# Totals in two rounded passes, maxima spread ahead of them, and table work one place forward, in the batch loop of a Perceiver layer

## The reference, cut to what matters

```
kvx = einsum('bsi,oi->bso', cond, w_kv_x)            # cond: 512 rows a batch
kx, vx = split(kvx, 2, axis=-1)
kx = _ln(kx.reshape(b, sc, g, d), kxln_w, kxln_b)    # 8 heads of 128
xout = softmax(q k^T * scale) v                      # 16 query heads
```

```
w = lut[idx]                                         # gate, up and down
```

## Time and profile before

| | us |
|---|---|
| median of 3 runs (427.23 to 427.74) | 427.55 |
| the profiled execution's own time | 427.4 |
| its span, first to last instruction | 425.6 |
| TensorE busy in the span | 414.7 |
| VectorE busy | 347.2 |
| ScalarE busy | 248.8 |

### The profile page before, as it was taken

The page is one execution under the profiler, slowest core; times in us unless marked ns, Lnnn a source line. Parts: engine busy times, 40 slices in busy tenths (PEclk is TensorE's granted clock), DMA queues, the critical chain, the costliest instruction groups (busy, mean ns, idle before and its releaser), DMA issues.

```text
span 425.6 us, 6868 instructions
## 1 busy us (share of the span) xinstructions
PE 414.7 (97%) x2427; PEld 292.2 (69%) x2433; DVE 347.2 (82%) x699; ACT 248.8 (58%) x780; POOL 35.8 (8%) x58
## 2 busy tenths in 40 slices
PE   8999999999999999999999999999999999999897
PEld 3453455788885767778676686785486799837596
DVE  5889999987999899689899998978887787746831
ACT  2478898688547777748986677664505263220220
POOL 0010000040000001100001000010010004101000
PEclk9999999999999999999999999999999999999999
DMA  7599120500002015993554835688337979730000
GB/s 240 226 191 415 39 85 2 199 2 26 27 2 99 1 51 123 201 306 78 132 124 92 198 70 108 155 187 359 74 78 246 390 267 241 151 125 2 2 2 25
DMA packets 14591, 56.80 MB, mean 133 GB/s; under 512 B 1824, under 2 KB 2912, under 8 KB 13280
## 3 DMA queue, kind: packets, MB, share of 16 engines
q1 hardware_dynamic: 11104, 39.31, 25.3%
q0 software_dynamic: 3456, 17.11, 21.4%
HBM read 41.40 MB, written 0.26 MB: 98 GB/s over the span
## 4 chain that ended last, share of the span: by engine, by line
PE 74%; DVE 12%; issue 6%; DMA 4%; ACT 3%; POOL 1%; SPq 0%; DVEq 0%; ACTq 0%; POOLq 0%
PE PS L482 11%; PE PS L1817 10%; PE PS L453 8%; PE PS L454 8%; PE PS L455 8%; PE PS L1846 3%; PE PS L535 3%; PE PS L1287 3%; DMA lutw_dt.float<-luttmp_dt.float 2%; PE PS L1832 2%; DMA raw_dt.float<-in_wk_nat 1%; PE PS L492 1%; PE PS L1153 1%; PE PS L1135 1%; PE PS L1295 1%
## 5 line engine op out<-in xcount | busy, mean ns | idle before, releaser
L605 ACT ACTIVATE sq_dt.float<-PS 128x128 bf16<-128x128 f32 x256 | 67.0, 279 | 27.0 <-PE PS L455 20.5
L482 PE MATMUL PS<-s_dt.float,ctx_ring_dt.float 128*128 128x512 f32 x128 | 57.8, 593 | 0.0
L605 ACT ACTIVATION_READ_ACCUMULATOR sq_dt.float<-PS 128x1 f32 x256 | 53.6, 210 | 0.0
L453 PE MATMUL PS<-wkc_dt.float32r,ctx_hi_dt.float32r 128*128 128x512 f32 x128 | 51.5, 402 | 0.1
L454 PE MATMUL PS<-wkT_dt.float32r,ctx_hi_dt.float32r 128*128 128x512 f32 x128 | 50.0, 390 | 0.0
L455 PE MATMUL PS<-wkc_dt.float32r,ctxT_ring_dt.float32r 128*128 128x512 f32 x128 | 49.9, 390 | 0.0
L687 ACT ACTIVATE luttmp_dt.float<-low_bit_dt.float,vec_dt.float,small_dt.float 128x1536 f32<-128x1536 uint8 x24 | 38.5, 1654 | 8.5 <-DMA lutw_dt.float<-luttmp_dt.float 8.5
L1817 PE MATMUL PS<-wch_dt.float,xs_dt.float 128*128 128x512 f32 x96 | 42.0, 592 | 0.0
L482 PEld LDWEIGHTS PS<-s_dt.float,ctx_ring_dt.float 128*128 128x128 f32 x128 | 23.6, 190 | 23.6 <-issue 23.0
L700 POOL DMA_DIRECT2D lutw_dt.float<-luttmp_dt.float x21 | 18.2, 869 | 234.7 <-DVE luttmp_dt.float L694 234.7
L694 DVE SCALAR_TENSOR_TENSOR luttmp_dt.float<-idx_dt.float,luttmp_dt.float 128x1536 f32<-128x1536 uint8 x21 | 36.6, 1753 | 0.0
(11 more groups left out here) (304 smaller groups left out, 851.3 us busy)
## 6 DMA issues: line engine op xcount, KB each, us to landing
lutw_dt.float<-luttmp_dt.float POOLq DMA_DIRECT2D x21, 768.0 KB, 6.1
wch_dt.float<-in_chunks SPq DMA_DIRECT2D x5, 1024.0 KB, 7.9
ctxT_ring_dt.float<-in_ctxT SPq DMA_DIRECT2D x8, 512.0 KB, 3.4
ctx_ring_dt.float<-in_ctx SPq DMA_DIRECT2D x8, 512.0 KB, 3.9
keysT_dt.float<-in_ctxT SPq DMA_DIRECT2D x8, 512.0 KB, 7.0
keys_dt.float<-in_ctx SPq DMA_DIRECT2D x8, 512.0 KB, 8.0
zu_dt.float<-in_wproj SPq DMA_DIRECT2D x1, 2048.0 KB, 7.2
A_first_dt.float<-in_wproj SPq DMA_DIRECT2D x1, 2048.0 KB, 10.2
```

Source lines behind the costliest of these rows:

```text
L453: nc.tensor.matmul(o, x_hi, hi[:, c, :], start=c == 0, stop=False)
L482: last = nc.tensor.matmul(mix_bank(b, c), keysr[k][:, t, c * 128:c * 128 + 128], sS[k][:, t, :], start=t == 0, stop=t == KT - 1)
L605: last = nc.scalar.activation(sq[:, (4 * hf + g) * D:(4 * hf + g + 1) * D], key_bank(b, 2 * t + hf)[:, g * D:(g + 1) * D], ACT.Square, acc ...
```

## The change

Totals: for batches 1 to 5 the fp32 product with ones becomes two `fp32r` products, of a rounded part `ps_hi` that ScalarE makes and of the rest `ps_lo` that VectorE makes. On TensorE the maxima of steps 2 to 6 are spread before the totals; in step 1 the order stays. On VectorE the sums go ahead of the split of the queries, the subtraction for `ps_lo` takes the place of the first table term, and that term goes behind the shift. GpSimd makes a rounded copy of the ones. Table work: step 1 takes four leaves and terms, steps 2 and 3 three each, step 4 two, and steps 5 to 7 as before.

```diff
-                    total(b - 1)
-                    spread(b)
+                    if isinstance(b, int) and b == 1:
+                        total(0)
+                        spread(1)
+                    else:
+                        spread(b)
+                        total(b - 1)
...
             def total(b):
-                pe.wait_ge(psum_ready, b + 1)
+                split = not (isinstance(b, int) and b in (0, 6, 7))
+                if split:
+                    pe.wait_ge(ps_split, b)
+                else:
+                    pe.wait_ge(psum_ready, b + 1)
...
+                if split:
+                    nc.tensor.matmul(bank(2), ones_r, ps_hi, start=True, stop=False)
+                    nc.tensor.matmul(bank(2), ones_r, ps_lo, start=False, stop=True).then_inc(sum_full, 1)
+                    return
                 nc.tensor.matmul(bank(2), ones, ps2[:, 0, :], start=True, stop=True).then_inc(sum_full, 1)
...
@@ ScalarE, step
-                    for m in range(3):
-                        leaf(act, b - 1, m)
+                    leaf(act, *LUT_TERMS[b][0])
+                    leaf(act, *LUT_TERMS[b][1])
+                if 1 < b < 7:
+                    hi_of_sum(b - 1)
+                for place in LUT_TERMS[b][2:3]:
+                    leaf(act, *place)
                 if prev and more:
                     inverse(b - 1)
+                for place in LUT_TERMS[b][3:]:
+                    leaf(act, *place)
                 if next_context:
                     split_context(b + 2, k)
...
+            def hi_of_sum(b):
+                act.wait_ge(psum_ready, b + 1)
+                nc.scalar.activation(ps_hi, ps2[:, 0, :], ACT.Copy).then_inc(ps_hi_ready, 1)
...
+        LUT_TERMS = {b: [(b - 1, m) for m in range(3)] for b in range(5, 8)}
+        LUT_TERMS[0] = []
+        LUT_TERMS[1] = [(0, 0), (0, 1), (0, 2), (1, 0)]
+        LUT_TERMS[2] = [(1, 1), (1, 2), (2, 0)]
+        LUT_TERMS[3] = [(2, 1), (2, 2), (3, 0)]
+        LUT_TERMS[4] = [(3, 1), (3, 2)]
...
+            pool.wait_ge(ld_const, 16)
+            nc.gpsimd.tensor_copy(ones_r, ones).then_inc(ones_ready, 1)
...
@@ VectorE, step
+                sums(b - 1, 1 - k)
                 if b > 1:
                     lo_of_A(dve, b + 1)
-                sums(b - 1, 1 - k)
                 maxima(b)
                 if b == 1:
                     lo_of_A(dve, 2)
-                term(dve, b - 1, 0)
+                else:
+                    lo_of_sum(b - 1)
                 shift(b, k)
+                term(dve, *LUT_TERMS[b][0])
                 normalise(b - 1, 1 - k)
...
-                term(dve, b - 1, 1)
+                term(dve, *LUT_TERMS[b][1])
...
-                term(dve, b - 1, 2)
+                for place in LUT_TERMS[b][2:]:
+                    term(dve, *place)
...
+            def lo_of_sum(b):
+                dve.wait_ge(ps_hi_ready, b)
+                nc.vector.tensor_tensor(ps_lo, ps2[:, 0, :], ps_hi, ALU.subtract).then_inc(ps_split, 1)
```

More of the change, by code:

```diff
@@ L70 @@
     ("vecs", 5 * NK, LOOP, LAST, "raw"), ("ctx_hi1", CT * NK, LOOP, LAST, "raw"),
+    ("ps_lo", NK, LOOP, LAST, "catc"), ("ps_hi", NK, LOOP, LAST, "raw"),
     ("keys", B * KT * C, TAIL, LATE, "catc"),
@@ L80 @@
     ("rotact", 4 * 1024, LATE, LATE), ("probs", 2 * TT * NK, LATE, LATE),
+    ("ones_r", 128, FRONT, LAST),
 ]
@@ L137, in build @@
         for name in ("zu", "catc", "lutw", "wkc", "wkT", "ctx_hi0", "ctx_hi1", "ctxT_ring", "A_hi", "A", "catx", "A_first", "beta", "gu_a", "gu_b", "gu_hi", "hT_hi",
-                     "hT_lo"):
+                     "hT_lo", "ps_hi", "ps_lo", "ones_r"):
             tensors[name, fp32r] = tensor(name, fp32r)
@@ L241, in build @@
             "st_full", "scaled", "sum_read", "mxf_ready", "tr_full", "m_ready", "mb_full"))
+        ps_hi_ready, ps_split, ones_ready = sem("ps_hi_ready"), sem("ps_split"), sem("ones_ready")
         shifted, p_ready, psum_ready, sum_full, r_ready, pctx, px_ready = (sem(n) for n in (
@@ L336, in build @@
         ps2 = buf("vecs", 2, 512, skip=1536)
+        ps_hi, ps_lo, ones_r = (buf(name, n, dtype=fp32r) for name, n in (("ps_hi", 512), ("ps_lo", 512), ("ones_r", 128)))
         px = buf("px", CT, NH, 64)
@@ L562, in loop_pe @@
             pe.wait_ge(ld_wvT, 16)
+            pe.wait_ge(ones_ready, 1)
             scores(1, 1, range(2))
```

## The result

| | before | after |
|---|---|---|
| median of 6 timed runs, us | 427.18 | 434.35 |
| lowest and highest of the runs compared | 426.58 to 427.74 | 432.40 to 435.68 |
| the profiled execution's own time | 427.4 | 432.4 |
| its span | 425.6 | 430.4 |

The changed kernel is slower: ratio 1.0155, 95% interval 1.0133 to 1.0176. One of the six runs after is not in that comparison: it took 532.12 us at a mean granted clock of 0.752; it is in the median, which is 433.75 without it. The profiled execution is the shortest of the others.

A forecast was written before the change was run, and what follows sets the result against it. TensorE was taken as the bound, busy 414.7 of 425.6 us. The terms 5.0 - 2.0 - 0.5 + 0.9 gave +3.4 us, +4.5 with the clock's 1.1, so a median of 432.1 us; range 430.0 to 434.2.

The forecast's parts named there:

- The fourth leaf, +5.0 us: Step 1: the leaf waits on ScalarE for the term behind the shift, delaying batch 2's squares and TensorE: +5.0 us.
- The clock, +1.1 us: Step 1: TensorE's clock falls through 5.2 us of idleness; from 0 to 2.1 us, taken as +1.1 us.
- Totals, -0.40 us a step: Steps 2 to 6: two rounded passes take 0.46 us instead of 0.86, saving 0.40 us each, -2.0 us together.
- Step 4, -0.5 us beside the totals: End of step 4: VectorE loses a term, gains a subtraction, and TensorE's 0.54 us of idleness goes: -0.5 us.
- Step 6, +0.9 us: Step 6: `normalise` stands behind the term, so TensorE waits anew ahead of the values of batches 4 and 5: +0.9 us.
- A stall at a full clock: Rival, step 1: TensorE waits as forecast but keeps its full clock; 431.0 us, chance 0.34.
- VectorE late in steps 3 and 5: Rival: VectorE's delay there reaches the scores, 0.56 us in both steps, +1.1 us; 433.2 us, chance 0.12.
- the short wait on ScalarE: Rival, step 1: the term is done by the time the inverse is; -1.6 us, 426.0 us, chance 0.12.

The follow-up runs named there:

- the second set: The changed kernel run again with nothing edited, beside other kernels on one chip: 433.51 us against 427.36 before, ratio 1.0147.
- the clock held: The changed kernel with 20 added matmuls that nobody reads on TensorE ahead of step 1's wait for the squares: 431.27 us, ratio to before 1.0096.
- `normalise` first: The changed kernel with three leaves and terms in each of steps 1 to 7, and `normalise` ahead of each step's first term: 427.75 us, ratio to before 1.0008.
- the two later sets: The kernel before the change, run beside the follow-up kernels on two chips: 427.33 and 427.36 us.
- the two kernels without a wait in steps 1 to 6: Three leaves and terms per step, `normalise` before the term, two pieces of the weights' split moved to step 7: 425.07 us; the same with fp32 totals: 427.12 us.

## Why the prediction was right

The forecast was 432.1 us for the median with 430.0 to 434.2 around it, and 431.9 for the profiled execution. That execution took 432.4. The median of the runs compared, 433.75, and that of the second set, 433.51, are inside; the first median over all six, 434.35, is 0.15 above the upper end. The mechanism came as forecast: one leaf, the squares behind it, TensorE's stall and the fall of the clock. One term was mis-sized, the clock's, and one came out by luck, step 4's. Point by point, by the ledger:

- *The fourth leaf, +5.0 us.* Right, in place and size. The third half tile was to start at 143.91 and started at 143.57, with the whole step 0.35 us earlier; 5.18 us of idleness against 5.2. One instruction in a queue carried the whole result: undoing the table takes it away, half undoing it (the term ahead of the shift) takes 2.2 us of it. With the clock held, "1 to 2" is 4.98 us longer than before: that is the stall alone.
- *The clock, +1.1 us.* It falls, as I took it; the size was too small. The ledger gives 1.76 and 1.55 us in two profiles, and the timed medians are 2.2 us apart (433.51 against 431.27, on two chips whose medians of before agree within 0.03). The step that failed is "part of it may pass before TensorE starts again": I halved the launch's 2.1 us without a row for the half, and 1.76 and 1.55 us of it fell on products. The comparison was weak besides: the launch was called the one longer idleness, but its row has 1.1 us of it, and what lies before the span is not in the trace. The Trainium skill (TensorE: Matmul & The Clock Gate, Why this matters for your kernels) says that idle gaps between bursts put the engine back to its lower rate; the trace agrees, with 0.43 us per product behind 5.18 us of idleness against 0.23 before it. It does not hold for every gap: behind 2.98 us the profile of the kernel with the term ahead of the shift has full speed.
- *Totals, -0.40 us a step.* Right: -0.43, -0.42 and -0.41 in steps 2, 3 and 5, and +0.41 or +0.42 when they are put back. The passes themselves take 0.54 us and not the 0.46 forecast; the key product behind them then holds TensorE for 0.24 us (167.59 to 167.83) instead of the 0.32 before (161.52 to 161.84), so the saving is as it was taken. The copy took 0.62 us, near the 0.64 of the nearest row.
- *Step 4, -0.5 us beside the totals.* Right as a number (-0.88 in all, against -0.9), and that is luck. The wait was to go; it cost 0.84 us, not the 0.54 of its bracket, and 0.39 us of it is left. VectorE's key scales come 0.85 us earlier in their step (21.81 us after the first mixing product, 22.66 before), not 1.06, and TensorE comes earlier too. What I did not see is what that edit does in this company: without it step 4 would wait 1.77 us, since the two passes load VectorE and hurry TensorE. The table with two terms there saves 26.61 - 24.94 = 1.67 us against its neighbour, not 0.5. That is why my numbers for two of the experiments were 2 us too low.
- *Step 6, +0.9 us.* A wait of 0.78 us where it was expected; with the totals' gain the step was to lose 0.5 us net and lost 0.64. `normalise` ahead of the term gives 1.03 us back.
- *The rivals.* A stall at a full clock is excluded by the slow products. VectorE late in steps 3 and 5 did not come: "3 to 4" and "5 to 6" are shorter than before. Nor did the short wait on ScalarE: 3.38 us. Two slips in the text change nothing here: the 0.65 us in the earlier trace rows is by its bracket a wait for ScalarE's squares, not for TensorE, and the range's lower end is the first rival (the stall at a full clock) without step 6's wait, 431.0 - 0.9 = 430.1, not the second.

On step 4 the reading of the kernel before was wrong too: VectorE does not wait for TensorE "in every step". Its key scales of step 4 have no bracket in the earlier trace rows, and its shift there has none either:

```profile
215.32 2.29 DVE L854 TENSOR_TENSOR s_dt.float<-s_dt.float,PS 128x2048 f32<-128x2048 f32 x1
```

Sum: +6.1 in step 1, -1.2, -0.9 and +0.5 were +4.5; measured +6.74, -1.26, -0.88 and +0.64, which is +5.24 in the loop. The span shows +4.8, since the first mixing product came 0.35 us earlier (126.87 against 127.22), and the profiled execution +5.0, with 2.0 us around the span instead of the 1.8 that was taken over. The timed medians show more, +6.15 us on the second chip (433.51 against 427.36). The profiled run was the shortest of its set there too; what the other five runs had on top, 0.3 to 1.2 us, stays open, since they have no trace.

## What to carry to other kernels

Where an in-order queue holds both a wait and the work that the bottleneck needs next, follow the wait back through the other engine's queue to its own releaser: here the leaf waited for a term that the same change had put behind the shift, and the price was the sum of the durations along that chain, to a tenth of a microsecond. An engine that the bottleneck waits for, be it 0.5 us at the end of a step, has no room: making the bottleneck faster and that engine's step longer adds both to the wait. A product's row without a bracket does not yet say that such a wait is gone; its weight load and its distance from the product ahead of it do. And move such work into waits that the same engine has elsewhere, read from the brackets of its timeline, before taking work from one full step into another.

## What was not expected of the hardware

Whether the clock falls behind a wait is not the same from run to run. Two profiles show it at the same place, the end of step 4. With the table work as before, the clock fell behind 1.77 us of waiting (5.29 us for the mixing products, above). With `normalise` first, it did not behind 1.75 us:

```profile
231.91 0.50 PE L461 MATMUL PS<-A_hi_dt.float32r,ctx_hi_dt.float32r 128*128 128x512 f32 x1 [1.75 <-DVE s_dt.float L771]
...
233.41 3.59 PE L490 MATMUL PS<-s_dt.float,ctx_ring_dt.float 128*128 128x512 f32 x8
```

The timed runs have a mean clock only, which does not say where it fell. The longest wait of TensorE in steps 1 to 6, and the runs whose mean clock was below 1.0, by 0.004 or more: 0.54 us, 5 of 47 (before, the two later sets); 1.75 to 1.77 us, 9 of 24; 2.98 us, 5 of 7; 5.18 us, all 11 that are compared. None was below with the wait of step 1 filled (6 runs), and 1 of 24 in the two kernels without a wait in steps 1 to 6, which is too near the 5 of 47 to tell from it. A profile at a full clock, such as that of the kernel with the term ahead of the shift, does not show what the timed runs pay.

The start moves too. The first mixing product of step 1 starts between 126.68 and 128.37 us in profiles of kernels that do not differ ahead of it. The waits of TensorE ahead of 20 us in the kernel with the clock held, the latest of them:

```profile
PE PS L1937 <- DMA raw_dt.float<-in_wk_nat: 1.4, 1, 1.4
PE PS L1837 <- POOL sq_dt.float L2078: 1.1, 1, 1.1
PE PS L1843 <- DVE raw_dt.float L2101: 0.8, 1, 0.8
```

and in the changed kernel:

```profile
PE PS L1835 <- POOL sq_dt.float L2076: 1.1, 1, 1.1
PE PS L1841 <- DVE raw_dt.float L2099: 0.9, 1, 0.9
PE PS L1935 <- DMA raw_dt.float<-in_wk_nat: 0.2, 1, 0.2
```

The wait for the first weights is 1.4 us in one and 0.2 in the other, which is most of the 1.5 us by which their loops start apart; the kernel that starts earliest, at 126.68, has no such wait there. Differences of a microsecond between two kernels are to be read from the loop, not from the span. What makes those loads late in some executions stayed open.
